# Causal attention with q and k as two float32r parts, two heads side by side in the array, and row maxima running ahead

## The chip, the cores and the metric

One core of a Trainium2 chip runs the whole program. The metric is the device time of one execution in microseconds (us); the kernel before takes 4158.48 us as the median of three runs (4147.53 to 4164.63). PE is TensorE (PEld its weight loads), DVE is VectorE, ACT is ScalarE, POOL is GpSimd, SP the engine whose queue issues nearly all DMAs.

## The reference

Two layers, each `x = x + attention(LN(x)) * silu(ffn(LN(x)))`, on 4 x 2048 tokens of width 256, 16 heads of dimension 16. Layer 0 has dilated, segmented attention and an FFN with fp8 rounding. Layer 1, which the change touches, is:

```python
q, k = _apply_rope(q, k, sin, cos)            # after q = x @ wq.T + bq, and so on
att = jnp.einsum('bhtd,bhsd->bhts', q, k) * (1.0 / np.sqrt(hd))
att = jnp.where(causal[None, None], att, -jnp.inf)
att = jax.nn.softmax(att, axis=-1)
y = jnp.einsum('bhts,bhsd->bhtd', att, v)
return jnp.einsum('btc,dc->btd', y.transpose(0, 2, 1, 3).reshape(B, T, C), wo) + bo
```

Its FFN is a mixture of 8 experts, the top 2 for each token, hidden width 1024. All of it is float32, and the kernel keeps nearly that precision.

## The kernel before

Four phases run one after the other: `layers_phase` (layer 0, and layer 1's norm, q, k, v and router logits, in 16 turns of 512 tokens), `attend_phase` (layer 1's attention), `experts_phase` and a final phase.

**layers_phase.** q and k come out of the rotation in `rot`, and are split into three bf16 pieces whose sum is the float32 value: ACT copies `rot` to piece 0 (`part0`, L565), DVE writes `rot` minus piece 0 back to `qk` (`rest`, L788), ACT copies that to piece 1 (`part1`, L569), POOL subtracts for piece 2 (`last_part`, L345). `store_layer1` writes the pieces to DRAM (L279) in 12 DMAs a turn. Between these, DVE works through the layer 0 part of the next token block: `residual` ends with `x1 = x + ez` (L773), then come norm statistics (L665), quantisation, the block-diagonal keys (L712 to L717, on which PE's `scores` wait).

**attend_phase.** 16 groups (4 batches x 4 quarters of the heads), G = 4 heads each, 2048 tokens. `qs` and `ks` hold, on 96 partitions, six stacked combinations of the pieces (`Q_PIECES`, `K_PIECES`), so that one bf16 matmul over 96 rows gives q times k at float32 precision; three more rows of `qs` hold minus the row maximum, also in three pieces, against ones in `ks`. Each group has two kinds of work:

- *Row scores* (`row_scores`, L1197, causal mask by an identity matmul L1200): queries on partitions, up to 512 keys. Only their maximum is used: DVE reduces each of the 160 chunks of a group (`chunk_max`, L1313) from `p1`, three buffers of one PSUM bank. At the end of the group `negate`, a PE transpose (L1206) and `split` turn the 64 x 128 maxima and split them into three pieces, and three DMAs (`maxima`, L1127) put them under the q rows.
- *Key scores* (`key_scores`, L1217, mask L1220): keys on partitions, queries along the row, in 20 steps of up to two key tiles, a head at a time (80 units) into `st`, two buffers of 1024 columns. ACT takes the exponential of each unit (L1294) into `ex`; the values matmuls (`values`, L1234, float32, the four heads in four column strips of 32) add the sums into `ob`; at each of the four query quarters' ends ACT copies `ob` (L1283), PE turns it (L1244), DVE divides (`normalise`, L1338 and L1341) into one of two `yout` buffers, SP stores it (L1135).

PE's order is written out: while group g does its key scores, the row scores of group g+1 are spread among them by `due_at`, a table from cumulative widths, and values lag one step. The maxima of g+1 are therefore complete only at g's end. The first group's 160 chunks run alone beforehand. SP's queue runs in program order; per group it holds the load of group g+2 (`load`, L1117 and L1120, 24 + 2 DMAs), three stores, the maxima, a fourth store. `normalise` waits until the store of two quarters before has landed.

## Time and profile before

| | us |
|---|---|
| median of three runs | 4158.48 |
| span of the profiled execution | 4106.3 |
| layers_phase | 0 to about 1110 |
| attention's own set-up and first load | about 1110 to 1161 |
| row scores of group 0 alone | 1161 to 1265 |
| 16 groups | 1265 to about 3098 |
| experts and final phase | to the end |

The profile shows one execution. Its span runs from the first to the last instruction; its own total time isn't recorded apart, and the median of the runs lies 52.2 us above the span. Busy times count overlapping instructions of one engine once; a matmul's duration includes the array's latency, so what a matmul costs in a dense stretch is the distance from one start to the next.

### The profile page before, as it was taken

The page shows a single profiled execution, that of the slowest core. Times are in us where ns is not written, and L with a number is a line of the kernel's source. Part 1 is how long each engine was busy: PE and PEld are TensorE (multiplying, and loading weights), DVE is VectorE, ACT ScalarE, POOL GpSimd, SP SyncE. Part 2 cuts the span into 40 slices and gives each one's busy share as a digit, 9 for nine tenths or more (in the row PEclk, how much of TensorE's full clock was granted, in tenths as well). Part 3 has the DMA queues.
Part 4 walks back from the last instruction along what each step waited for, and adds up shares of the span by engine and source line. Part 5 has one row for each costly group of instructions (what it writes and reads, how often), then busy time and mean ns, then how long its engine had stood idle before and what let it go on. Part 6 is the DMA issues. An engine that isn't in the chain of part 4 may idle for free. (4 is left out here: it accounts for less than half of the span.)

```text
span 4106.3 us, 65569 instructions
## 1 busy us (share of the span) xinstructions
PE 3499.3 (85%) x20499; PEld 1877.5 (46%) x20500; DVE 2863.1 (70%) x5100; ACT 1766.9 (43%) x2274; POOL 745.4 (18%) x968
## 2 busy tenths in 40 slices
PE   5777777777359999999999999999997999999954
PEld 2333333343113333333333333333335888888943
DVE  5777776776468777788778778787724665566556
ACT  2333333333103665666566566566673332233211
POOL 0333323233112222100000000000002121111066
PEclk9899888888658999999999999999998999999977
DMA  2121221212232221123333212223002121121077
GB/s 70 45 79 57 67 83 41 82 51 68 78 75 45 48 47 35 25 41 47 48 46 48 48 26 41 39 41 48 7 7 90 58 71 61 66 67 62 32 204 215
DMA packets 261897, 247.41 MB, mean 60 GB/s; under 512 B 92530, under 2 KB 233970, under 8 KB 261306
## 3 DMA queue, kind: packets, MB, share of 16 engines
q1 hardware_dynamic: 245178, 209.58, 21.8%
q0 software_dynamic: 16384, 33.64, 2.8%
q8 instruction: 175, 2.87, 0.3%
q14 instruction: 160, 1.31, 0.1%
HBM read 149.70 MB, written 92.67 MB: 59 GB/s over the span
## 5 line engine op out<-in xcount | busy, mean ns | idle before, releaser
L1313 DVE TENSOR_REDUCE at_part<-at_p 128x1 f32<-128x512 f32 (+3 forms) x2560 | 1402.1, 605 | 310.4 <-PE at_p L1197 192.2
L1294 ACT ACTIVATE at_ex<-at_st 128x1024 f32<-128x1024 f32 (+1 forms) x1280 | 1109.3, 895 | 830.8 <-PE at_st L1220 472.5
L1197 PE MATMUL at_p<-at_ks,at_qs 96*128 96x512 bf16 (+3 forms) x2560 | 838.3, 366 | 89.6 <-DVE at_part L1313 32.8
L1217 PE MATMUL at_st<-at_qs,at_ks 99*128 99x512 bf16 (+3 forms) x2560 | 713.3, 350 | 6.5 <-ACT at_ex L1294 4.9
L1234 PE MATMUL at_ob<-at_ex,at_vs 128*32 128x512 f32 (+3 forms) x5120 | 588.3, 541 | 3.6 <-ACT at_ex L1294 3.5
L1197 PEld LDWEIGHTS at_p<-at_ks,at_qs 96*128 96x128 bf16 x2560 | 248.1, 98 | 688.5 <-DVE at_part L1313 490.4
L1475 POOL DMA_INDIRECT e_xg<-s_xn,e_table x128 | 146.9, 1148 | 1978.2 <-DMA e_table<-s_table 1405.2
L1565 ACT ACTIVATE e_hh<-e_hb,e_b1now 128x512 fp32r<-128x512 f32 x256 | 176.3, 689 | 527.5 <-PE e_hb L1500 498.9
L1217 PEld LDWEIGHTS at_st<-at_qs,at_ks 99*128 99x128 bf16 x2560 | 242.0, 99 | 252.2 <-ACT at_ex L1294 97.8
L1530 PE MATMUL e_ob<-e_w2h,e_hh 128*128 128x256 f32 x1024 | 295.1, 288 | 15.5 <-DVE e_og L1623 15.5
L1532 PE MATMUL e_ob<-e_w2h,e_hl 128*128 128x256 f32 x1024 | 291.7, 285 | 0.0
L1531 PE MATMUL e_ob<-e_w2l,e_hh 128*128 128x256 f32 x1024 | 291.5, 285 | 0.0
L1608 DVE TENSOR_SCALAR e_h<-e_hb,e_b1now 128x512 f32<-128x512 f32 x256 | 191.1, 746 | 57.6 <-ACT e_hh L1565 54.5
L1200 PE MATMUL at_p<-at_mask_q,at_identb 128*128 128x128 bf16 x1024 | 231.1, 228 | 0.0
L598 ACT ACTIVATE a_wexp<-a_shifted 128x512 f32<-128x512 f32 x128 | 80.6, 630 | 329.5 <-DVE a_shifted L726 329.5
L423 PE MATMUL a_sc<-a_qT,a_kbd 128*128 128x512 f32 x256 | 162.9, 736 | 64.3 <-DVE a_vbd L717 63.1
L1623 DVE TENSOR_TENSOR e_og<-e_ob,e_b2now 128x256 f32<-128x256 f32 x128 | 53.7, 424 | 231.7 <-PE e_ob L1532 231.1
L1498 PE MATMUL e_hb<-e_xh,e_w1h 128*128 128x512 f32 x512 | 203.4, 397 | 6.0 <-issue 3.7
L1530 PEld LDWEIGHTS e_ob<-e_w2h,e_hh 128*128 128x128 f32 x1024 | 196.5, 192 | 17.0 <-DVE e_og L1623 17.0
L1500 PE MATMUL e_hb<-e_xh,e_w1l 128*128 128x512 f32 x512 | 203.0, 397 | 0.0
L1499 PE MATMUL e_hb<-e_xl,e_w1h 128*128 128x512 f32 x512 | 202.9, 396 | 0.0
L1220 PE MATMUL at_st<-at_mask_k,at_identb 128*128 128x128 bf16 x1024 | 200.4, 223 | 0.0
(180 smaller groups left out, 4706.9 us busy)
## 6 DMA issues: line engine op xcount, KB each, us to landing
s_qk<-a_piece SPq DMA_DIRECT2D x192, 128.0 KB
at_qs<-s_qk SPq DMA_DIRECT2D x192, 128.0 KB
at_ks<-s_qk SPq DMA_DIRECT2D x192, 128.0 KB
s_v<-a_v SPq DMA_DIRECT2D x64, 256.0 KB, 5.5
at_vs<-s_v SPq DMA_DIRECT2D x32, 512.0 KB
e_w<-w SPq DMA_DIRECT2D x16, 1024.0 KB, 7.5
s_eo<-e_og SPq DMA_DIRECT2D x32, 512.0 KB, 2.6
a_x<-x SPq DMA_DIRECT2D x16, 512.0 KB, 5.2
```

Of the source, the lines that this page charges most:

```text
L1197: last = pe.matmul(out, qs[0:STACK, r, h, qt * P:(qt + 1) * P], ks[0:STACK, r, h, ch * SEG:ch * SEG + w], start=True, stop=not diag)
L1200: last = pe.matmul(out[:, w - P:w], identb[:], mask_q[:], start=False, stop=True)
L1217: last = pe.matmul(out, ks[:, r, h, kt * P:(kt + 1) * P], qs[:, r, h, q0:q0 + w], start=True, stop=not diag)
L1234: last = pe.matmul(ob[h * HW:(h + 1) * HW, SEG - w:SEG], vs[:, r, kt, h * HW:(h + 1) * HW], ex[:, (G * s + h) % NE, at:at + w], start=(kt ...
L1294: ev.done(act.activation(ex[:, u % NE, 0:width], st[:, u % 2, 0:width], ACT.Exp, scale=SCALE), "ex")
L1313: ev.done(dve.tensor_reduce(part[:, at, ch:ch + 1], p1[:, n % NP1, 0:w], AX, ALU.max), "mx")
L1498: pe.matmul(out, ah, bh, start=(j == 0), stop=False)
L1499: pe.matmul(out, ah, bl, start=False, stop=False)
L1500: last = pe.matmul(out, al, bh, start=False, stop=(j == len(pairs) - 1))
L1530: pe.matmul(out, high, w2h[:, u, m, :], start=(m == 0), stop=False)
L1531: pe.matmul(out, high, w2l[:, u, m, :], start=False, stop=False)
L1532: last = pe.matmul(out, low, w2h[:, u, m, :], start=False, stop=(m == HC - 1))
```

## The change

q and k become two float32r parts instead of three bf16 pieces: ACT copies `rot` to part 0, DVE writes `rot` minus part 0 straight to part 1; `part1` and `last_part` are gone. They are stored in 8 DMAs a turn, in a layout with a head's 16 rows together. Loads become 12 + 2 DMAs of 16 rows.

In attention, three stacked combinations (48 rows) plus two rows for the maxima lie at partitions 0 and again at 64, for two heads (a = 0, 1) of a pair; two matmuls, one on rows 0 to 63 and one on rows 64 to 127, follow one another and write different PSUM banks. Masks are matmuls of 64 rows and 64 columns, four for each pair of diagonal tiles instead of two of 128. DVE reduces both heads of a pair with one instruction (up to 128x1024, L1365), from two buffers of two banks; key scores have three buffers of one bank and steps of one key tile (36 steps, 144 exponentials of up to 512 columns instead of 80 of up to 1024), `ex` sixteen buffers. Row maxima are turned a query quarter at a time and run ahead of use: group g's stream holds its own last quarter (0, 3) and the next group's quarters (1, 0), (1, 1), (1, 2), 80 pair chunks and four transposes, and only three quarters of group 0 run alone beforehand. Maxima reach `qs` in eight DMAs a quarter. Values lag one step (two at a quarter's start), and the last values, turn and normalise of group g run in the first two steps of g+1. In SP's queue the last store of group g-1 now stands behind the load of group g+2.

```diff
+        NBUF, NE, NST, NP1 = 3, 4 * G, 3, 2
+        p1 = ps("p1", [P, NP1, PAIRS, SEG])
+        so = ps("so", [P, NST + 1, SEG])
...
+        lead = stream([(0, 0), (0, 1), (0, 2)], [None, (0, 0), (0, 1)])
+        run = stream([(0, 3), (1, 0), (1, 1), (1, 2)], [(0, 2), (0, 3), (1, 0), (1, 1)])
+        tail = stream([(0, 3)], [(0, 2)]) + [("t", 0, 3)]
...
+                def group(g, r, use, first, more):          # SP
+                    items = run if more else tail
+                    maxima(r, 2, g, LEAD + turned_at(items, 0, 2))
+                    if first:
+                        load(slice(2, 3), 2)
+                    else:
+                        if not isinstance(g, int) or g + 2 < NGROUPS:
+                            ev.wait(sp, "pv", g, 0)
+                            sp.sem_inc(passed, 1)
+                            load(bass.ds(g + 2, 1), (r + 2) % NBUF)
+                        output(g - 1, 3)
+                    output(g, 0)
+                    output(g, 1)
+                    maxima(r, 3, g, LEAD + turned_at(items, 0, 3))
...
+                def add_mask(out, mask, a, half, last):
+                    rows = slice(a * HALF, (a + 1) * HALF)
+                    return pe.matmul(out[:, half * HALF:(half + 1) * HALF], mask[rows, half, :], identb[rows, rows],
+                                     start=False, stop=last)
...
+                    for a in range(2):                      # row_scores
+                        rows = slice(a * HALF, a * HALF + STACK)
+                        last = pe.matmul(p1[:, b, a, 0:w], qs[rows, r, p, qt * P:(qt + 1) * P],
+                                         ks[rows, r, p, ch * SEG:ch * SEG + w], start=True, stop=not diag)
...
+                        for a in range(2):                  # key_scores
+                            if i == 0 and (not first or v + a >= NST):
+                                ev.wait(pe, "ex", g, v + a - NST + 1)
+                            rows = slice(a * HALF, a * HALF + ROWS)
+                            last = pe.matmul(so[:, (v + a) % NST, at:at + w], ks[rows, r, p, kt * P:(kt + 1) * P],
+                                             qs[rows, r, p, q0:q0 + w], start=True, stop=not diag)
...
-                def last_part(st, n):
-                    st.mark(pool.tensor_tensor(piece[2][:], qk[:], piece[1][:], ALU.subtract), "p3", n)
-                    st.mark(dve.tensor_tensor(qk[:], rot[:], piece[0][:], ALU.subtract), "rest", n)
+                    st.mark(dve.tensor_tensor(part[1][:], rot[:], part[0][:].bitcast(F32), ALU.subtract), "p2", n)
```

PE in the middle of a group, before: a unit of two key tiles of one head (L1217), single row chunks (L1197), one tile of values (L1234, each row two passes for four heads).

```order
L1217 MATMUL at_st<-at_qs,at_ks 128x512 x2
L85 REGISTER_ALU
L1197 MATMUL at_p<-at_ks,at_qs 128x512
L1200 MATMUL at_p<-at_mask_q,at_identb 128x128
L1234 MATMUL at_ob<-at_ex,at_vs 32x512 x4
L85 REGISTER_ALU
L1197 MATMUL at_p<-at_ks,at_qs 128x512
L85 REGISTER_ALU
L1217 MATMUL at_st<-at_qs,at_ks 128x512
```

PE in the middle of a group, now (L1267 key scores, L1233 row scores, x2 being the two heads of a pair, L1223 masks, L1287 values):

```order
L1267 MATMUL at_so<-at_qs,at_ks 128x512 x2
L1233 MATMUL at_p<-at_ks,at_qs 128x512 x2
L1287 MATMUL at_so<-at_ex,at_vs 32x512 x4
L1267 MATMUL at_so<-at_qs,at_ks 128x512 x2
L1233 MATMUL at_p<-at_ks,at_qs 128x512 x2
L1267 MATMUL at_so<-at_qs,at_ks 128x512 x2
L1233 MATMUL at_p<-at_ks,at_qs 128x512 x2
L1223 MATMUL at_p<-at_identb,at_key_mask 128x64 x4
L1287 MATMUL at_so<-at_ex,at_vs 32x512 x4
```

One tile of values now stands behind two key pairs and two or three row pairs. SP's queue for one group, before (L1135 are the stores, L1127 the maxima):

```order
L1117 DMA at_qs<-s_qk 8x4x2048 x12
L1117 DMA at_ks<-s_qk 8x4x2048 x12
L1120 DMA at_vs<-s_v 128x8x128 x2
L1135 DMA s_y<-at_yout 128x4x64 x3
L1127 DMA at_qs<-at_mT 1x64x128 x3
L1135 DMA s_y<-at_yout 128x4x64
```

SP's queue for one group, now (L1154 maxima, L1141 and L1144 the load, L1160 stores):

```order
L1154 DMA at_qs<-at_mT 1x4x128 x8
L1141 DMA at_qs<-s_qk 16x2x2048 x6
L1141 DMA at_ks<-s_qk 16x2x2048 x6
L1144 DMA at_vs<-s_v 128x8x128 x2
L1160 DMA s_y<-at_yout 128x4x64 x3
L1154 DMA at_qs<-at_mT 1x4x128 x16
L1160 DMA s_y<-at_yout 128x4x64
```

The store that closed a group's rows before is the first of the three behind the load now. DVE in group 0 now, with what it waits for (L1383 begins `normalise`; a group's second one waits for the `yout` buffer that the last store of the group before reads):

```order
L1365 TENSOR_REDUCE at_best<-at_p 128x2 [waits at_s1] x8
L1383 RECIPROCAL at_rden<-at_so 128x16 [waits at_y_out0,at_ot]
L1386 TENSOR_TENSOR at_yout<-at_so,at_rden 128x256 [waits at_rden]
L1365 TENSOR_REDUCE at_best<-at_p 128x2 [waits at_s1] x15
L1383 RECIPROCAL at_rden<-at_so 128x16 [waits at_y_out1,at_ot]
L1386 TENSOR_TENSOR at_yout<-at_so,at_rden 128x256 [waits at_rden]
```

The fifteen reduces between the two are row pairs; the second `normalise` stands in step 11 of 36.

## Rows read from the trace of the kernel before

**Rows 1.** The page: span, and busy time of each engine.

```profile
span 4106.3 us, 65569 instructions
PE 3499.3 (85%) x20499; PEld 1877.5 (46%) x20500; DVE 2863.1 (70%) x5100; ACT 1766.9 (43%) x2274; POOL 745.4 (18%) x968
```

**Rows 2.** Stretches: length, busy us of PE, PEld, DVE, ACT, POOL; clock, DMA share.

```profile
1161.00:1265.00 104.00, 80.82 (x225) 21.24 (x225) 97.80 (x188) 0.00 (x0) 23.85 (x43) 0.50 0.16 38
1500.00:1900.00 400.00, 385.11 (x2711) 153.54 (x2710) 318.45 (x604) 245.57 (x291) 56.43 (x100) 0.99 0.28 47
3010.00:3098.00 88.00, 80.14 (x588) 24.21 (x584) 3.02 (x10) 70.44 (x87) 0.00 (x0) 1.00 0.03 7
```

**Rows 3.** One instruction per group: the maxima's cast, first and last start.

```profile
L1326 DVE CAST at_mT<-at_p x16: 282/283/283, 1260.4 to 3007.1; 64x128 bf16<-64x128 f32 x16
```

**Rows 4.** Timeline of PE in attention and in the experts: start, us, instruction.

```profile
3003.28 0.38 PE L1217 MATMUL at_st<-at_qs,at_ks 99*128 99x512 bf16 x1
3003.50 0.22 PE L1220 MATMUL at_st<-at_mask_k,at_identb 128*128 128x128 bf16 x1
3003.56 0.33 PE L1217 MATMUL at_st<-at_qs,at_ks 99*128 99x384 bf16 x1
...
3004.48 1.07 PE L1234 MATMUL at_ob<-at_ex,at_vs 128*32 128x512 f32 x8
3005.48 0.39 PE L1217 MATMUL at_st<-at_qs,at_ks 99*128 99x512 bf16 x1
...
3300.22 0.39 PE L1498 MATMUL e_hb<-e_xh,e_w1h 128*128 128x512 f32 x1
3300.45 0.40 PE L1499 MATMUL e_hb<-e_xl,e_w1h 128*128 128x512 f32 x1
```

**Rows 5.** DVE's timeline: routing work amid group 0's chunks, one head's 40 chunks.

```profile
1163.56 1.22 DVE L986 COPY r_count<-at_st 128x1024 f32<-128x1024 f32 x1
...
1176.71 19.74 DVE L1313 TENSOR_REDUCE at_part<-at_p 128x1 f32<-128x512 f32 x38
1196.63 20.88 DVE L1313 TENSOR_REDUCE at_part<-at_p 128x1 f32<-128x384 f32 x40 [0.17 <-PE at_p L1200]
```

**Rows 6.** By shape, 1265 to 3007 us: busy, mean ns of one, idle before.

```profile
L1313 DVE TENSOR_REDUCE at_part<-at_p 128x1 f32<-128x512 f32 x1680 | 1096.8, 685 | 226.1 <-PE at_p L1197 191.7 <-PE at_p L1200 25.3
L1294 ACT ACTIVATE at_ex<-at_st 128x1024 f32<-128x1024 f32 x959 | 957.7, 1023 | 677.3 <-PE at_st L1217 343.1 <-PE at_st L1220 325.8
L1283 ACT ACTIVATE at_osb<-at_ob 128x512 f32<-128x512 f32 x59 | 35.0, 593 | 10.6 <-PE at_ob L1234 10.6
```

**Rows 7.** SP's queue in one group, then DMA share and GB/s of its load.

```profile
2541.07 1.77 SPq L1127 DMA_DIRECT2D at_qs<-at_mT  x3
...
2547.70 4.91 SPq L1117 DMA_DIRECT2D at_qs<-s_qk  x12
...
2557.78 27.58 SPq L1120 DMA_DIRECT2D at_vs<-s_v  x2
...
2548.00:2600.00 52.00, 50.43 (x354) 20.22 (x352) 43.83 (x83) 33.19 (x40) 0.00 (x0) 1.00 0.61 89
2568.00:2572.00 4.00, 4.00 (x32) 1.83 (x30) 3.10 (x6) 2.71 (x3) 0.00 (x0) 1.00 0.52 75
```

**Rows 8.** layers_phase: L773's ns min/median/max, and POOL beside the 4.7 us one.

```profile
L773 DVE TENSOR_TENSOR a_x<-a_x,a_ez x16: 1224/4691/4704, 78.8 to 1047.5; 128x1024 f32<-128x1024 f32 x16
725.46 4.70 DVE L773 TENSOR_TENSOR a_x<-a_x,a_ez 128x1024 f32<-128x1024 f32 x1
725.00 4.08 POOL L345 TENSOR_TENSOR a_piece<-a_qk,a_piece 128x2048 bf16<-128x2048 f32 x1 [17.27 <-DMA s_qk<-a_piece]
```

**Rows 9.** First load and first chunk; a stretch behind 12.5 us without matmuls, granted clock.

```profile
1116.60 4.06 SPq L1117 DMA_DIRECT2D at_qs<-s_qk  x12
1161.23 0.29 PE L1197 MATMUL at_p<-at_ks,at_qs 96*128 96x128 bf16 x1 [31.18 <-DMA at_vs<-s_v]
1058.80:1066.90 8.10, 6.83 (x14) 3.75 (x15) 0.00 (x0) 1.77 (x3) 0.00 (x0) 0.50 0.70 218
```

More of the change, by code:

```diff
@@ L1066, in attend_phase, with quarter @@
-        due_at = [min(u for u in range(TURN_AT) if step_work[u + 1] * chunk_work[-1] >= c * step_work[-1])
-                  for c in chunk_work]
-        def due(u):
-            return [n for n in range(NC) if due_at[n] == u]
-        counts = dict(s1=NC, mx=NC, neg=1, negT=1, mT=1, m_in=PIECE, st=NU, ex=NU, pv=NS, oc=SPB, ot=SPB,
+        NV = NS * G
+        ends = [max(s for s in range(NS) if steps[s][0] == qc) for qc in range(SPB)]
+        starts = [0] + [s + 1 for s in ends[:-1]]
+        def quarter(ahead, qc):
+            return [("c", ahead, qc, p, qt, ch) for qt in range(TT * qc, TT * qc + TT)
+                    for ch in range(qc + 1) for p in range(PAIRS)]
@@ new lines, in stream @@
+        def stream(quarters, turned):
+            out = []
+            for (ahead, qc), t in zip(quarters, turned):
+                chunks = quarter(ahead, qc)
+                out += chunks[:2] + ([("t",) + t] if t else []) + chunks[2:]
+            return out
+        lead = stream([(0, 0), (0, 1), (0, 2)], [None, (0, 0), (0, 1)])
+        run = stream([(0, 3), (1, 0), (1, 1), (1, 2)], [(0, 2), (0, 3), (1, 0), (1, 1)])
+        tail = stream([(0, 3)], [(0, 2)]) + [("t", 0, 3)]
+        LEAD, RUN = len(lead), len(run)
@@ new lines, in wide, with due @@
+        def wide(item):
+            return min(SEG, (item[4] + 1) * P - item[5] * SEG) if item[0] == "c" else P // 2
+        FIXED = P // 2
+        step_work = np.cumsum([0] + [steps[u // 2][1][-1][1] + steps[u // 2][1][-1][2] + FIXED for u in range(2 * NS)])
+        item_work = np.cumsum([wide(x) + FIXED for x in run])
+        slot_of = [min(u for u in range(2 * NS) if step_work[u + 1] * item_work[-1] >= w * step_work[-1])
+                   for w in item_work]
+        def due(u, more):
+            return [k for k in range(RUN if more else len(tail)) if slot_of[k] == u]
@@ new lines, in closes, with turned_at, summed_after, sums_after @@
+        def closes(items, k):
+            return items[k][0] == "c" and not any(x[:3] == items[k][:3] for x in items[k + 1:])
+        def turned_at(items, ahead, qc):
+            return items.index(("t", ahead, qc)) + 1
+        def summed_after(s):
+            return s + 2 if s in starts else s + 1
+        def sums_after(s):
+            return [x for x in range(NS) if summed_after(x) == s]
+        counts = dict(s1=RUN, mx=RUN, neg=SPB, mstep=SPB, m_in=G * PART * SPB, st=NV, ex=NV, pv=NS, oc=SPB, ot=SPB,
@@ L1139, in _ @@
                 route.zero_table(sp)
-                maxima(0, 0)
-                def turn(i, loads):
-                    for r in range(NBUF):
-                        g = i * NBUF + r
-                        if r < loads:
-                            ev.wait(sp, "pv", g, 0)
-                            sp.sem_inc(passed, 1)
-                            load(bass.ds(g + 2, 1), (r + 2) % NBUF)
-                        group(g, r, True)
-                NTURN = (NGROUPS - 1) // NBUF
-                with sp.Fori(0, NTURN - 1) as i:
-                    turn(i, NBUF)
-                turn(NTURN - 1, NBUF - 1)
-                group(NGROUPS - 1, 0, False)
+                for qc in range(2):
+                    maxima(0, qc, 0, turned_at(lead, 0, qc))
+                groups(sp, group)
+                output(NGROUPS - 1, 3)
                 for k in range(2):
@@ new lines, in stream_item @@
+                def stream_item(g, r, use, it, n, items, k):
+                    item = items[k]
+                    if n + k >= NP1:
+                        ev.wait(pe, "mx", it, n + k - NP1 + 1)
+                    if item[0] == "c":
+                        if item[1] == 1 and item[1:] == quarter(1, 0)[0][1:]:
+                            ev.wait(pe, f"in{(r + 1) % NBUF}", use, 1)
+                        last = row_scores((r + item[1]) % NBUF, item, (n + k) % NP1)
+                    else:
+                        ev.wait(pe, "neg", g + item[1], item[2] + 1)
+                        last = pe.transpose(p1[:, (n + k) % NP1, 0, 0:P], negmax[:], ident[:])
+                    ev.done(last, "s1")
@@ L1233, in values @@
+                def values(g, r, s):
+                    qc, tiles = steps[s]
+                    ev.wait(pe, "ex", g, G * s + G)
+                    if s in starts:
+                        ev.wait(pe, "norm", g, qc)
+                    for kt, at, w in tiles:
                         for h in range(G):
@@ L1235, in values @@
                                              ex[:, (G * s + h) % NE, at:at + w], start=(kt == 0),
[L1236 to L1239 removed]
+                                             stop=(s in ends and kt == tiles[-1][0]), skip_group_check=True)
+                    ev.done(last, "pv")
                 def turn(g, qc):
@@ L1269, in _ @@
                 route.prefix_sums(pe)
                 ev.wait(pe, "in0", 0, 1)
-                for n in range(NC):
-                    row_scores(0, 0, n)
-                turn_maxima(0)
-                group_loop(pe, group)
+                for k in range(LEAD):
+                    stream_item(0, 0, 0, 0, 0, lead, k)
+                groups(pe, group)
+                values(NGROUPS - 1, (NGROUPS - 1) % NBUF, NS - 1)
+                turn(NGROUPS - 1, SPB - 1)
             @block.scalar
```

377 lines of the change are left out of this document (174 added, 203 removed).

## Prediction

> **What bounds the kernel now.** I read the page first, then a table of stretches, then attention's timeline by engine. The page gives PE 85%, DVE 70%, ACT 43% of 4106.3 us [rows 1], an average over phases with different limits. The stretches tell more: in the group loop PE is busy 385 of 400 us, DVE 318, ACT 246 [rows 2]. The cast that ends each group's maxima starts at 1260.4 us the first time and at 3007.1 the sixteenth [rows 3], so a group takes (3007.1 - 1260.4)/15 = 116.4 us. A busy PE isn't proof, so I price its work by the distance between starts [rows 4]: a 512-column bf16 matmul 0.22 us, a 128-column mask 0.06, one values tile for four heads 1.00 until the next matmul. A group has 224 full score matmuls (48.4 us at 0.216), 96 narrower ones at 0.16, 0.11 and 0.06 (10.6), 128 masks (7.7), 40 values tiles (28 full, 12 narrow, with the gap ahead of each some 38), and four turns at about 0.65 (2.6). That is 107 us of 116.4: PE's own work is the bound, and 9 us go to waits on its neighbours.
>
> **Attention's loop, engine by engine.** All a group's scores are now pairs on two halves of the rows: 112 full pairs and 48 narrow ones. float32r streams 512 columns in 0.23 us [rows 4]; no row of before shows two halves side by side. If they run side by side a full pair costs 0.23, otherwise 0.46. I take side by side, because the values matmuls already do it by columns: eight instructions, two passes each for four heads, end within 1.07 us [rows 4], where one after the other 8 x 0.427 would be 3.4. So 112 x 0.232 = 26.0, and 48 x 0.2 = 9.6 for the narrow ones (between 0.06, a mask's spacing, and 0.23). The 256 quarter masks have no row of their shape: between 0.03 (half of 0.06) and 0.06 each is 7.7 to 15.4; I take 11.5. Values keep 29.0 us of streaming (17,408 columns x 4 passes at 2.4 GHz), with 0.23 around each of 36 calls instead of 40: 37.3. Turns and the four maxima transposes: 3.8. PE's sum is 88 us.
>
> DVE: one head's 40 chunks took 20.88 us back to back [rows 5], so 83.5 a group. A 1024-wide read of PSUM is 1.22 alone, a full chunk 0.685 [rows 5, 6], so 128 columns are 0.134, and from 20.88 a full chunk in a row is (20.88 + 3.2)/40 = 0.60. A full pair in a row is then 1.14. With 56 full pairs (63.6) and 24 narrow ones at 0.87, 0.60 and 0.34 (14.5) the maxima cost 78; normalise, negating and splitting by quarter add 6. DVE's sum is 84. ACT: 128 exponentials of 512 columns, 0.593 as L1283's copy and 0.57 in a row [rows 6], 16 of 256 at 0.35, four copies: 81.
>
> Three engines at 88, 84 and 81 that wait on each other can't reach the largest sum. PE is in order and has to come back to the key pair. A head's second matmul of step s needs the exponential of the first (three buffers), so one step can't be shorter than: key pair to its end 0.40 [rows 4], exponential 0.57, second key pair 0.23, half of the step's row chunks, values 1.08 with the gap. Without the chunks that is 2.28 x 36 = 82; half the row chunks' PE time (13.0 + 4.8 full and narrow, 5.8 masks, 1.2 transposes) adds 12.4, the key masks in twelve steps 3, turns 2.6, less 2 for narrow steps: 98, and since a step has one to five chunks, unevenly, I round up to **100 us a group**, against 116.4.
>
> **A new wait.** `normalise` of quarter 1 stands at the end of step 11 and needs the store of the previous group's quarter 3, which SP now issues behind the load. Step 11 ends after 32.5% of the widths, so at 0.325 x 100 + 1 = 33.5 us. The load: the first transposed maxima are ready at about 4.3 us (step 1), eight DMAs at 0.59 [rows 7] make 8.7. The load now takes 52 us at a DMA share of 0.61, that is 31.7 us of all sixteen engines; while q and k move the share is 0.52 [rows 7], half the engines, with 8 partitions to a DMA. With 16 partitions I take 31.7. The store lands about 3 us behind it, at 43.4. DVE waits 10 us, and behind it in its queue are the row chunks, for which PE waits after two buffers, and ACT after PE. After such a pause PE runs at the lower of its two levels: behind 12.5 us without matmuls it had granted clock 0.50 (1.2 GHz) for 8 us [rows 9]. I add 3 us for that. A group then takes **113 us**, and the loop gains 15 x (116.4 - 113) = 51. The Trainium skill ("DMA: Bandwidth & Descriptors", section on why a DMA increments its semaphore by 16) says that a DMA uses the largest number of engines up to 16 that divides its slowest dimension: 8 before and 16 now. The 0.52 agrees; by the page the load would indeed need half the time for q and k.
>
> **The rest.** *Lead.* From the first chunk to the first key scores it is 1161.2 to 1265.4 = 104 us, DVE-bound (97.8 of 104) [rows 2]. Now 13.1 us of routing work [rows 5], 48 pair items (24 full at 1.14, 24 diagonal in fours of 1.14, 0.87, 0.60, 0.34: 45), 5 for negating, splitting and short bubbles: 63, minus 41. PE is at 0.50 there, where a full pair is 0.43, under DVE's 1.14. *layers_phase.* L773 takes 1.22 us alone and 4.69 in the median, when POOL's L345 runs beside it [rows 8]; L345 is gone. DVE has no idle time from there to the block-diagonal keys, for which PE waits, so 14 turns x 3.4 count: minus 48. ACT's second copy (1.9 us) stood in idle time: nothing. *Its end.* One ACT copy, L345 (4.1) and four DMAs fewer, less what larger DMAs cost: minus 6. *First load.* 1116.6 to 1161.2 = 44.6 [rows 9] becomes 32 + 2, but the three memsets and the ones by DMA start it 3 later: minus 8. *Last group.* 88 us before [rows 2], with PE 80 and ACT 70; the same step chain gives about 88: nothing.
>
> Sum: 51 + 41 + 48 + 6 + 8 = 154; 4106.3 - 154 = 3952. The median of the runs lies 52.2 above the profiled span, so **4004**, say 4000.
>
> **Rivals.**
> *The store's wait doesn't bite* (the load drains faster, or slack in buffers takes it): 100 us a group, 15 x 16.4 = 246 + 103 = 349, giving 3809. For it: a stretch of layers_phase moved 218 GB/s [rows 9], the load 89. Against: the stores stand in order behind 4 MB.
> *The halves don't run side by side.* Pairs cost 33 us more, PE 121, with 7 to 9 of waits 129 a group: +189, the last group +10, -103: 4255, **slower**. It decides from 0.38 us for a full pair on (PE's sum then 105 to 110 and a group above 123). For it: no row shows row halves. The Trainium skill ("TensorE: Matmul & The Clock Gate", "Measured speedup vs the span model") gives 3.07 times for four row tiles, so it speaks against this rival; by it a pair would be close to 0.23.
> *The load keeps its 52 us pace.* The store lands at 8.7 + 52 + 3 = 64, DVE waits 30 us, a group takes up to 133 with the clock's 3: 4300 at most, **slower**; it decides from about 40 us of load on, where a group takes 121 to 124. For it: 512-byte rows of v hold the queue 27.6 us even now [rows 7].
> *Tighter coupling*: bursts of three narrow chunks with masks in one step and two values tiles in another; 106 instead of 100: 4060.
> *The change doesn't do what it says* would show as pairs in sequence, the second rival. That PE falls to 1.2 GHz for the whole loop, as in the lead at 0.50 with PE waiting for each chunk [rows 2], would cost hundreds; I give it 3%.
>
> **How the numbers follow.** 4000 has 0.42, the first rival 0.24, tighter coupling 0.08, faster than all 0.04; halves in sequence 0.11, the slow load 0.08, the clock 0.03. The forecast's own range is 3930 to 4060. 3770 to 4180 leaves out the worst of the slow cases and the fastest. Faster by more than 0.5% (what a measurement can tell here) 0.79, same 0.05, slower 0.16.
>
> **What would show it.** Pairs of L1267 and L1233 starting within hundredths of each other, pairs 0.23 apart; L1365 at 1.14 us; the spacing of the maxima casts about 113; once a group, near a third of it, an idle stretch of 8 to 12 us on DVE ahead of L1383 that a store ends, and the clock low behind it; L773 at 1.2 in every turn; a lead of 63. Wrong would be: pairs 0.46 apart, no such idle stretch, or a DMA share that stays at 0.5.

## The result, and the profile after

The changed kernel takes 4312.5 us (median of 4 runs, 4277.1 to 4321.2) against 4161.6 us for the kernel before in the same set: ratio 1.035, 95% interval 1.030 to 1.040. It is **slower by 3.5%**; 4000 us had been forecast, with 3770 to 4180 as the range. In a later set, on another chip, the ratio was 1.026 (1.023 to 1.029).

The page of the changed kernel: span, busy time, then PE's busy share and the granted clock in 40 slices [beside rows 1]. The profiled execution's own time is 4277.1 us.

```profile
span 4275.2 us, 67161 instructions
PE 3545.4 (83%) x22596; PEld 2019.3 (47%) x22596; DVE 2761.8 (65%) x3918; ACT 1788.8 (42%) x3282; POOL 678.5 (16%) x952
...
PE   5777777875498998999998898889987999999745
...
PEclk9899998997579998778779999996987999999867
```

No engine has a higher busy share than before, and in the loop the clock goes down to 7 tenths where it was 0.99 [rows 2]. Next, one source line each (ns min/median/max, first and last start): DVE's addition in layers_phase, row pairs, key pairs.

```profile
L761 DVE TENSOR_TENSOR a_x<-a_x,a_ez x16: 1224/1224/1226, 79.0 to 1010.2; 128x1024 f32<-128x1024 f32 x16
L1233 PE MATMUL at_p<-at_ks,at_qs x2560: 215/436/793, 1107.0 to 3145.2; 48*128 48x512 f32 x137, 48*128 48x128 f32 x20, 48*128 48x384 f32 x20, 48*128 48x256 f32 x20
L1267 PE MATMUL at_so<-at_qs,at_ks x2560: 275/494/793, 1169.6 to 3217.9; 50*128 50x512 f32 x139, 50*128 50x384 f32 x20, 50*128 50x256 f32 x19, 50*128 50x128 f32 x19
```

These date every part. The first row chunk starts at 1107.0 instead of 1161.2 [rows 9], the first key pair at 1169.6 instead of 1265.4: **95.8 us gained** before the loop. From the first key scores to the last the kernel before needs 1265.4 to 3094.7, 1829.3 us; now it is 2048.3: **219 us lost** in the loop, 187 of them in the fifteen stretches of the next section, 17 ahead of these and 15 behind. What follows attention is the same code in both and took 46 us longer here, nearly all in the last phase. As far as the sets tell, that goes by the chip: they fall into chips with the kernel before at 4162 to 4178 us and the time behind the last `normalise` at 1046 to 1064, and chips with 4109 to 4120 and 1005 to 1019. The profile of before, with 1009, fits the latter. -96 + 219 + 46 = 169, the difference of the two spans.

### The profile page after: what moved, and what is told of

The parts are those of the page before. It is cut to its first block and busy times, and to the rows that moved or that the text cites. A ratio compares the mean times of both kernels' runs of the same rounds, so it can differ in the third digit from the quotient of the medians.

```text
span 4275.2 us, 67161 instructions
## 1 busy us (share of the span) xinstructions
PE 3545.4 (83%) x22596; PEld 2019.3 (47%) x22596; DVE 2761.8 (65%) x3918; ACT 1788.8 (42%) x3282; POOL 678.5 (16%) x952
## 5 line engine op out<-in xcount | busy, mean ns | idle before, releaser
L1365 DVE TENSOR_REDUCE at_best<-at_p 128x2 f32<-128x1024 f32 (+3 forms) x1280 | 1336.8, 1064 | 557.7 <-PE at_p L1233 372.5
L1341 ACT ACTIVATE at_ex<-at_so 128x512 f32<-128x512 f32 (+1 forms) x2304 | 1164.1, 576 | 962.5 <-PE at_so L1267 560.6
L1267 PE MATMUL at_so<-at_qs,at_ks 50*128 50x512 f32 (+3 forms) x2560 | 854.1, 492 | 95.5 <-ACT at_ex L1341 68.8
L1233 PE MATMUL at_p<-at_ks,at_qs 48*128 48x512 f32 (+3 forms) x2560 | 709.6, 460 | 106.6 <-DVE at_best L1365 62.4
L1267 PEld LDWEIGHTS at_so<-at_qs,at_ks 50*128 50x128 f32 x2560 | 382.1, 205 | 738.3 <-ACT at_ex L1341 546.0
L1287 PE MATMUL at_so<-at_ex,at_vs 128*32 128x512 f32 (+3 forms) x5120 | 671.7, 621 | 36.7 <-DVE at_yout L1386 36.4
L1233 PEld LDWEIGHTS at_p<-at_ks,at_qs 48*128 48x128 f32 x2560 | 325.4, 210 | 152.7 <-DVE at_best L1365 108.0
L1569 PE MATMUL e_ob<-e_w2h,e_hh 128*128 128x256 f32 x1024 | 293.6, 287 | 15.6 <-DVE e_og L1662 15.6
L1287 PEld LDWEIGHTS at_so<-at_ex,at_vs 128*32 128x32 f32 x5120 | 124.7, 117 | 251.0 <-issue 154.9
L712 DVE TENSOR_REDUCE a_keymax<-a_sc 128x8 f32<-128x512 f32 x128 | 88.2, 689 | 167.5 <-PE a_sc L417 166.0
L1570 PEld LDWEIGHTS e_ob<-e_w2l,e_hh 128*128 128x128 f32 x1024 | 195.1, 191 | 0.0
```

The costliest lines, as they stand in the source:

```text
L1233: last = pe.matmul(p1[:, b, a, 0:w], qs[rows, r, p, qt * P:(qt + 1) * P], ks[rows, r, p, ch * SEG:ch * SEG + w], start=True, stop=not diag)
L1267: last = pe.matmul(so[:, (v + a) % NST, at:at + w], ks[rows, r, p, kt * P:(kt + 1) * P], qs[rows, r, p, q0:q0 + w], start=True, stop=not diag)
L1287: last = pe.matmul(ob[h * HW:(h + 1) * HW, SEG - w:SEG], vs[:, r, kt, h * HW:(h + 1) * HW], ex[:, (G * s + h) % NE, at:at + w], start=(kt ...
L1341: ev.done(act.activation(ex[:, v % NE, 0:width], so[:, v % NST, 0:width], ACT.Exp, scale=SCALE), "ex")
L1365: ev.done(dve.tensor_reduce(best[:, at:at + TT * PAIRS + 1:TT * PAIRS, ch], p1[:, (n + k) % NP1, :, 0:wide(item)], AX, ALU.max), "mx")
L1569: pe.matmul(out, high, w2h[:, u, m, :], start=(m == 0), stop=False)
```

## Where the loop's time goes

**Groups at different clocks.** A table of stretches, each from one group's third reciprocal (L1383, the start of a `normalise`) to the next one's, five of fifteen: length, busy us of PE, PEld, DVE, ACT, POOL, clock, DMA share, GB/s.

```profile
1643.10:1785.80 142.70, 132.05 (x919) 60.88 (x920) 89.09 (x101) 74.34 (x148) 12.05 (x21) 0.74 0.25 35
...
1917.10:2056.30 139.20, 129.32 (x918) 58.84 (x920) 88.69 (x100) 74.55 (x148) 0.00 (x0) 0.76 0.25 35
...
2319.50:2439.70 120.20, 107.68 (x919) 49.98 (x918) 88.13 (x101) 74.05 (x149) 0.00 (x0) 0.94 0.29 41
...
2562.80:2681.40 118.60, 105.62 (x919) 48.62 (x919) 88.09 (x102) 74.01 (x149) 0.00 (x0) 0.97 0.28 42
...
2801.10:2936.90 135.80, 124.11 (x918) 56.09 (x917) 88.84 (x101) 74.55 (x149) 0.00 (x0) 0.80 0.26 37
```

The same program takes 118.6 to 142.7 us, longer the lower the clock. The granted clock is 1.0 (2.4 GHz) or 0.5 (1.2 GHz), so a mean of 0.74 over 142.7 us is about 73 us at 1.2 GHz. Over all fifteen the mean is 127.5 us with 32.4 at 1.2 GHz; a straight line through the fifteen gives 115.6 + 0.37 for each low microsecond. I call 115.6 the full-clock group. Before, the fifteen average 115.1, the last, without row scores for a next group, included. So there are two losses to explain: full-clock groups that are no shorter than before, and 12 us a group for the clock.

**A step at the full clock.** PE, ACT and DVE in one step with two row chunks, one behind each key pair.

```profile
2585.61 0.50 PE L1267 MATMUL at_so<-at_qs,at_ks 50*128 50x512 f32 x2
...
2585.94 0.40 PE L1233 MATMUL at_p<-at_ks,at_qs 48*128 48x512 f32 x2
...
2586.14 2.07 ACT L1341 ACTIVATE at_ex<-at_so 128x512 f32<-128x512 f32 x4 [1.38 <-PE at_so L1267]
2586.18 0.40 PE L1267 MATMUL at_so<-at_qs,at_ks 50*128 50x512 f32 x1
2586.39 2.39 DVE L1365 TENSOR_REDUCE at_best<-at_p 128x2 f32<-128x1024 f32 x2 [0.97 <-PE at_p L1233]
2586.79 0.18 PEld L1267 LDWEIGHTS at_so<-at_qs,at_ks 50*128 50x128 f32 x1 [0.65 <-ACT at_ex L1341]
2586.79 0.50 PE L1267 MATMUL at_so<-at_qs,at_ks 50*128 50x512 f32 x1 [0.21 <-ACT at_ex L1341]
...
2586.88 0.64 PE L1233 MATMUL at_p<-at_ks,at_qs 48*128 48x512 f32 x2
...
2587.44 1.06 PE L1287 MATMUL at_so<-at_ex,at_vs 128*32 128x512 f32 x8
2588.44 0.19 PEld L1267 LDWEIGHTS at_so<-at_qs,at_ks 50*128 50x128 f32 x2 [0.84 <-ACT at_ex L1341]
```

The first pair is side by side (x2, ended within 0.50 us). The second is not: its first half starts at 2586.18, its second at 2586.79, when the exponential of the step's first head frees the third buffer, and the row chunk behind it is pulled apart with it. Round the step: key pair to exponential 0.53, exponential and hand-over 0.65, second half of the key pair and of the chunk 0.65, values 1.00: **2.83 us**. DVE and ACT both idle in it.

**The load.** The load of one group in the table of stretches (columns as above), then PE's timeline in it.

```profile
1968.00:1976.00 8.00, 7.32 (x67) 3.78 (x59) 6.35 (x9) 5.14 (x11) 0.00 (x0) 1.00 0.64 91
1976.00:1994.00 18.00, 17.05 (x155) 7.40 (x155) 13.50 (x13) 11.51 (x25) 0.00 (x0) 1.00 1.04 121
1994.00:1998.20 4.20, 0.11 (x3) 0.03 (x2) 0.17 (x1) 1.51 (x3) 0.00 (x0) 0.72 0.96 103
1998.20:2010.00 11.80, 11.80 (x51) 5.52 (x50) 6.94 (x8) 4.54 (x9) 0.00 (x0) 0.50 0.48 111
2010.00:2040.00 30.00, 29.61 (x165) 12.84 (x162) 15.22 (x20) 12.05 (x24) 0.00 (x0) 0.50 0.00 1
...
2067.00:2090.00 23.00, 20.32 (x148) 8.19 (x148) 18.33 (x20) 14.61 (x29) 0.00 (x0) 0.99 0.01 2
...
1998.17 0.48 PE L1233 MATMUL at_p<-at_ks,at_qs 48*128 48x384 f32 x1 [4.09 <-issue]
```

PE stands 4.09 us between the two matmuls of one pair, where nothing in the program makes it wait ("issue"), and the clock is 0.50 from there to 2067, 72 us in all. What it waited for shows by DMA queue: the 25 us before the pause, and the 28 before those.

```profile
q1 hardware_dynamic: 536, 2.89, 95.0%
```

```profile
q8 instruction: 3, 0.05, 0.9%
q14 instruction: 2, 0.02, 0.2%
q1 hardware_dynamic: 40, 0.01, 0.2%
```

I read queue 8 as the one that brings PE's code: it moves blocks of 16 KB, mostly every 10 to 20 us. While q and k of the load take 95% of the sixteen engines none comes, for 26 us (1968.5 to 1994.8), and PE runs dry; the block of 1994.8 lands at 1996.6, and PE goes on at 1998.17. In the kernel before the load had 57% of the engines, and code blocks came. The Trainium skill ("DMA: Bandwidth & Descriptors", section "Queues, rings and completion order") has each engine take turns between the queues that have work for it; by that alone a block would not be held up for so long. The times here show that it is held up, though not to the load's end: v's 1 MB moved until 2006, with another block, at 2002.3, amid it. That the missing block is what PE waited for is inferred from these times; e16 below tests it. Two other things mark a group: the wait of normalise for the store, and PE's pause of 1.2 us in step 27 of all fifteen groups, where two 128-column chunks stand behind a full one and PE waits for DVE. And the pauses are not all of the clock's story: of the 486 us at 1.2 GHz in the fifteen stretches some 200 begin where PE has not stood for over 1 us, most of them in steps 4 and 15, three times for 41 us on end. For the wait of normalise, what ended the idle time before L1383 (us, times):

```profile
  DMA s_y<-at_yout: 44.0, 11
```

## The experiments

"Group" is the mean of the fifteen distances as above, "low" the part of it at 1.2 GHz, "full" the straight line's value at no low clock (left out where nearly every microsecond was low). Ratios are to the kernel before, measured in the same set; the sets ran on different chips, so ratios are compared, not times.

| kernel | ratio (95%) | group | low | full |
|---|---|---|---|---|
| changed | 1.035 (1.030 to 1.040) | 127.5 | 32.4 | 115.6 |
| e14_again, the same | 1.026 (1.023 to 1.029) | 129.9 | 41.0 | 115.1 |
| e1_store_first | 1.029, medians alone | 129.5 | 43.1 | 116.2 |
| e2_cols | 1.017 (1.010 to 1.023) | 126.9 | 45.7 | 106.4 |
| e4_double_first | 1.016 (1.012 to 1.020) | 122.9 | 13.2 | 114.7 |
| e6_same_half | 1.313 (1.305 to 1.321) | 206.2 | 179.3 | |
| e7_cols_store | 0.998 (0.993 to 1.002) | 122.7 | 37.7 | 106.8 |
| e8_cols_one | 1.040 (1.035 to 1.045) | 133.1 | 45.1 | 113.4 |
| e9_cols_both | 1.053 (1.049 to 1.057) | 136.5 | 36.0 | 120.0 |
| e11_spread | 1.017 (1.012 to 1.021) | 125.7 | 31.9 | 114.8 |
| e12_cols_spread | 1.013 (1.009 to 1.017) | 124.5 | 41.2 | 105.5 |
| e13_cols_early | 0.983 (0.979 to 0.986) | 117.8 | 27.6 | 102.5 |
| e16_after_six | 1.026 (1.022 to 1.029) | 128.4 | 44.0 | 112.8 |
| e18_place | 0.979 (0.973 to 0.985) | 113.1 | 9.6 | 109.0 |
| **e15_six** | **0.942 (0.940 to 0.943)** | 107.1 | 10.6 | 101.2 |
| e17_unroll | 0.942 (0.939 to 0.944) | 106.1 | 9.2 | 101.5 |

### Are the halves side by side? e6_same_half

```diff
-    rows = slice(a * HALF, a * HALF + STACK)     # row pairs; key pairs and masks alike
+    rows = slice(0, STACK)
```

> The changed kernel with both heads of every pair, and both mask halves, on the first 64 rows of the array, so that they run one after the other (this leaves out the second head's scores: its columns are computed from the first head's rows). If the halves run side by side in the changed kernel, each full pair now costs 0.43 to 0.46 instead of 0.23 to 0.33 where it doesn't wait: 10 to 25 us a group more, 4470 to 4700. Rival, they never overlapped in time although they start together: no difference, 4280 to 4340.

Ratio 1.313: the halves do run side by side in the changed kernel, and this rival of the prediction is dead. The loss, 79 us a group, is far above the 10 to 25 expected, since the clock was low nearly throughout. The stretch 1400 to 2600 of this kernel:

```profile
1400.00:2600.00 1200.00, 1187.32 (x5190) 633.22 (x5183) 510.39 (x569) 433.15 (x839) 67.73 (x120) 0.55 0.17 25
```

PE is busy 1187 of 1200 us, and the clock is 0.55. A PE that never stands can still be at 1.2 GHz.

### The step: e2_cols, and doubled work: e4_double_first, e8_cols_one, e9_cols_both

e2 cuts the 512-column values tile into two times 256 columns and puts one part between the step's key pairs. (It cuts a quarter's first tile too, and so leaves part of that tile's sums out; from e7 on that tile is whole.)

```diff
 for p in range(PAIRS):
     key_scores(g, r, s, p, first)
     for k in due(2 * s + p, more):
         stream_item(g, r, use, g, LEAD, items, k)
...
-for x in sums_after(s):
-    values(g, r, x)
+    for x, part in (halves[:cut], halves[cut:])[p]:
+        values(*x, part)
```

> The changed kernel with the values tile of a 512-column step cut into two times 256 columns, one between the step's two key pairs and one behind the second (in the five steps that hold a quarter's first tile everything stays behind). Return-path theory: the exponential of the first head is done by the time PE comes to the second key pair, both its halves start together, and a two-chunk step falls from 2.85 us to 2.2 to 2.4 at the full clock; a group from 116 to 98 to 104, and the whole to 3980 to 4130, with a clock above 0.87 since PE waits less. Rival, PE's own work is the bound of the step (PE is busy 90% of the stretch 2500 to 2700): 28 more matmul groups with a start of their own each make a group 0 to 5 us longer, 4310 to 4390.

The full-clock group fell from 115.6 to 106.4, so the wait for the exponential was the bound of a step, though the 98 to 104 expected weren't reached. And the low clock rose to 45.7 us and ate most of the gain: a group took 126.9 us, the whole 4236, above the expected range.

e4 computes a row pair twice where PE was thought to wait.

```diff
-    last = row_scores((r + item[1]) % NBUF, item, (n + k) % NP1)
+    for _ in range(times):      # 2 for the first chunk behind the first key pair
+        last = row_scores((r + item[1]) % NBUF, item, (n + k) % NP1)
```

> The changed kernel with the first row-score chunk behind the first key pair of each step computed twice (same output, 0.25 us of PE work more in nearly every one of 36 steps, 8 to 9 us a group). Return-path theory: it lies in the 0.61 us between the two halves of the second key pair, during which PE waits for the exponential, so the group stays within 3 us: 4290 to 4360. Rival, PE's sum is the bound: +8 to 9 us a group, 4440 to 4460. If it is too little PE activity that lets the clock fall, the clock rises above 0.87 here.

More work made it **faster** than the changed kernel, by 1 to 2% (1.016 against 1.026 and 1.035 in two sets), outside the range expected: free at the full clock (114.7 for 115.6), and the low clock down to 13.2 us. From this I took a simple theory, that the clock follows the amount of work, and tried it on the cut version.

> The same with the first row-score chunk behind the first key pair of each step computed twice, as extra work for PE (0.25 us, about 30 times a group; same output). Clock theory: the low clock falls from 40 to 55 us a group to 5 to 20, which gives back 10 to 18 us, against 4 to 7 us of added PE time in steps that DVE bounds: a group 111 to 118, the whole 4060 to 4140. Rival, work and clock are not tied (the doubled chunk helped the changed kernel in another way): the added work costs 30 x 0.25 = 7 us a group and the time rises by 100 over the run without it.

> The same with the first chunk behind each of the two key pairs of a step computed twice (about 65 of a group's 80 chunks). Clock theory: the clock is low for under 5 us a group, but now 14 to 16 us of PE time are added, and a half step becomes 0.5 + 0.34 + 0.33 + 0.25 = 1.4 us instead of 1.24: a group 117 to 122, the whole 4130 to 4200, slower than with one chunk doubled. Rival as above: 4330 or more.

It fell: one doubled chunk adds 7 us to the full-clock group, as priced, and the low clock goes up, not down (45.1 for 37.7 us; with two chunks doubled it is 36.0). The place of the falls says more than the sum of work. In e8 and e9 the clock falls behind pauses of PE in steps 7 to 10 (1.8 to 6.6 us, waiting for code), in step 27 (1.1 us) and at the loop's turn, and behind step 27 it stays low up to 61 us. Why doubling shortened these stretches in e4 and not here stays open.

### The store and the load: e1_store_first, e7_cols_store, e11_spread, e12_cols_spread, e16_after_six

```diff
-load(bass.ds(g + 2, 1), (r + 2) % NBUF)
 output(g - 1, 3)
+load(bass.ds(g + 2, 1), (r + 2) % NBUF)
```

> The changed kernel with one edit: in each group SP issues the store of the previous group's quarter 3 ahead of the load of the group after next. The wait of normalise (L1383) for that store, 44.0 us in 11 groups of the changed kernel's trace, should vanish, and with it PE's 36.4 us at the values matmuls. Return-path theory (the loop is slower because a step's second key pair waits for the exponential of its first, and because the granted clock falls): only these 36 to 44 us go, the clock stays near 0.86, 4312 becomes 4260 to 4280. Rival, the store wait as the root, whose pauses let the clock fall for the rest of the group: the low clock goes too (about 500 us of the loop at 1.2 GHz, which cost some 12 us a group), and the time comes to 4080 to 4130.

The wait for the store went wholly, the time hardly: median 4287.2 (4218 to 4321, too wide for an interval), 1.029 of the kernel before in its set, between the 1.026 and 1.035 of the changed kernel. The low clock stayed (43.1 us; its profile is of the run with 4321). With the cut values on top:

> The changed kernel with both edits so far: values of 512 columns cut in two, one part between the step's key pairs (a quarter's first tile stays whole and behind), and the store of quarter 3 ahead of the load. Clock theory (PE's granted clock falls the more, the less matmul work the array does per time): at the full clock a group takes 103 to 107 us as in the run with the cut values (106.4 extrapolated to no low clock), but 40 to 55 us of each group are at 1.2 GHz, so a group comes out at 122 to 127 and the whole at 4190 to 4240. Rival, the clock fell there because of the pauses at the store's wait: with these gone a group takes 105 to 112 and the whole 3980 to 4060.

0.998, 37.7 us of low clock: the store's pauses were not the root. Against e2 (1.017, 45.7) something was gained; how much of it comes from the store and how much from the whole first tile isn't separated. Next, v's halves apart from q and k, behind the stores of quarters 0 and 1, in the changed kernel and in the cut version.

> The changed kernel with one edit: the load of the group after next is no longer issued in one piece. q and k stay where they are, the first half of v goes behind the store of quarter 0, the second behind that of quarter 1, so the store of quarter 3 follows q and k at once. Theory (the load at a DMA share of 1.0 holds back PE's code and the store; PE stands 1.4 to 9.2 us in steps 11 and 12 of 13 groups, and each pause is followed by a stretch at the low clock): these pauses go, the low clock falls from 32 us a group to 12 to 20, a group from 127.5 to 118 to 122, and the ratio to before from 1.035 to 0.995 to 1.015. Rival, the clock falls from too little work in the array and the pauses only mark the place: the low clock stays at 28 to 40 us a group and only the pauses' 3 us go, ratio 1.02 to 1.03.

> The kernel with the cut values and the early store (122.7 us a group with 37.7 at the low clock, 106.8 extrapolated to none), with v loaded as two pieces in the same way. By the theory the pauses of 3.4 to 6.4 us in steps 7 to 10 go with the 20 us of low clock behind each; those of step 27 (0.8 us) and of the loop's turn stay: low clock 15 to 25 us, a group 112 to 117, ratio 0.955 to 0.975 instead of 0.998. Rival: unchanged clock, ratio 0.985 to 1.00.

Both missed; e12 is even above e7 (1.013 for 0.998). PE's pauses stayed (1.4 to 4.4 us in step 11; 2.8 to 6.8 in steps 7 to 10), since q and k alone still come in one burst: the code blocks are mostly 23 to 29 us apart there, and mostly 10 to 19 elsewhere. So the load in six pieces in the changed kernel, with the store of quarter 3 ahead of them (condensed):

```diff
+def piece(k):
+    load(bass.ds(g + 2, 1), (r + 2) % NBUF, [k])   # q, k of half 0, 1; v's halves
 maxima(r, 2, g, ...)
+output(g - 1, 3); piece(0)
-load(bass.ds(g + 2, 1), (r + 2) % NBUF)
-output(g - 1, 3)
-output(g, 0); output(g, 1)
+output(g, 0); piece(1); output(g, 1); piece(2)     # 3 to 5 behind the next three
```

> The changed kernel with one edit: the load is issued as six pieces of 0.5 or 0.75 MB (q of each half, k of each half, v's two halves) at six places of the group instead of at one, behind steps 2, 5, 12, 16, 20 and 23; the store of quarter 3 stands ahead of them. Theory (the load in one burst holds back PE's code and the store): no gap of over 20 us between two code blocks, no pause of PE over 1.4 us except at the loop's turn, step 27's 1.2 us stays; low clock 32 to 41 us a group becomes 12 to 22, a group 118 to 122, ratio to before 0.985 to 1.005 instead of 1.026 to 1.035. Rival (the clock falls for lack of work, wherever): pauses go but the low clock stays above 28 us, ratio 1.01 to 1.025.

Half right. The pauses of over 1 us in steps 3 to 26 of the fifteen groups are gone, so the load in one burst was their cause. Moving the store alone, as e1 and e7 do, had ended only those that wait for it. But the time is no better (1.026), and 44.0 us of a group are at the low clock: it falls in step 15 (12 times in 15 groups, against 4 in the changed kernel), 4 and 27, and stays down 3 to 55 us, most often 41. The stretches around one such step, and DVE in it:

```profile
1858.00:1866.00 8.00, 7.56 (x57) 2.80 (x56) 6.80 (x6) 4.87 (x10) 0.00 (x0) 1.00 0.84 116
1866.00:1869.00 3.00, 2.27 (x25) 1.35 (x21) 2.27 (x5) 2.07 (x4) 0.00 (x0) 0.94 0.00 0
1869.00:1895.00 26.00, 25.62 (x157) 11.94 (x159) 11.31 (x17) 9.86 (x20) 0.00 (x0) 0.50 0.24 36
...
1866.45 1.23 DVE L1374 TENSOR_REDUCE at_best<-at_p 128x2 f32<-128x1024 f32 x1 [0.52 <-PE at_p L1232]
1867.71 0.22 DVE L1379 TENSOR_REDUCE at_negmax<-at_best 128x16 f32<-128x64 f32 x1
1867.85 0.75 DVE L1374 TENSOR_REDUCE at_best<-at_p 128x2 f32<-128x256 f32 x2
1868.85 0.28 DVE L1384 CAST at_mT<-at_p 64x128 fp32r<-64x128 f32 x1 [0.25 <-PE at_p L1261]
...
1869.41 0.69 DVE L1374 TENSOR_REDUCE at_best<-at_p 128x2 f32<-128x512 f32 x1
```

Step 15 has a full chunk, two of 128 columns, a transpose and one of 256 in a row. Two buffers tie PE to DVE's pace there, so PE has a few narrow matmuls in 3 us, and the clock falls at the end.

### Work beside the narrow chunks: e13_cols_early, e18_place

```diff
-    for k in due(2 * s + p, more):
+    mine = due(2 * s + p, more)
+    for k in mine[:1]:
         stream_item(g, r, use, g, LEAD, items, k)
...
+    for k in mine[1:]:
+        stream_item(g, r, use, g, LEAD, items, k)
```

> As the one before, and in each half step the values part stands behind the first row chunk instead of behind all of them, so that PE has work while DVE reads a wide chunk ahead of narrow ones (step 27: PE waited 0.8 us there in each group of the loop, and the low clock began behind it in 8 of 15 groups and lasted up to 51 us). By the theory the falls at step 27 go: low clock under 15 us, a group 108 to 113, ratio 0.94 to 0.96. Rival, a pause of 0.8 us is not what lets the clock fall: low clock as in the one before, difference under 0.5%.

No clock falls at step 27 are left but one at 28 in group 0, and the ratio goes from 1.013 to 0.983 (low 41.2 to 27.6 us, less than hoped: the load's pauses were still there). e18 does the same to e16, with the values whole:

> The changed kernel with the load in six pieces (ratio 1.0255, 128.4 us a group, 44.0 of them at the low clock, 112.8 extrapolated to none) and one more edit: a step's values stand whole behind the first row chunk of its second key pair instead of behind all chunks (in steps 27 and the like, with three chunks behind the first key pair, behind the first of these). Theory (the clock falls where the narrow chunks come one behind the other with PE waiting for DVE between them): the falls in steps 15 and 27 go, the low clock comes to 5 to 18 us a group, a group to 113 to 119, ratio 0.97 to 0.995. Rival, only the cut values (fewer waits of the key pair for the exponential) keep the clock: low clock above 30 us, ratio 1.01 to 1.03.

Low clock 44.0 to 9.6 us, ratio 1.026 to 0.979, within the range expected; no fall in step 15, two left from step 28, and short ones (3 to 17 us) in step 20. **It was the place of the values**, behind the first chunk, where they give PE work while DVE reads. (The full-clock group fell too, from 112.8 to 109.0.)

### Both together: e15_six and e17_unroll

> The version with cut values behind the first row chunk (117.8 us a group, 27.6 of them at the low clock, ratio 0.983, 102.5 extrapolated to none), with the load in six pieces. Theory: the pauses of 3 to 6 us in steps 7 to 10 of 11 groups go and with them 14 to 24 us of low clock each: low clock 5 to 12 us a group, a group 105 to 110, ratio 0.935 to 0.96. Rival: low clock stays above 22 us, ratio 0.97 to 0.985.

> As e15_six, with PE's 16 groups written out instead of a loop over three groups at a time, so that PE's program has no jump. Theory: PE's pauses of 2.7 to 3.3 us at the loop's turn (groups 3, 6, 9) and the 14 us of low clock behind each are gone: 4 x (3 + 5) = 20 to 30 us less than e15_six. Rival: without the loop the code comes no sooner, difference within 10 us.

3881.8 us against 4120.4: **5.8% faster than the kernel before**, some 8 to 9% faster than the changed one. Its page and a two-chunk step:

```profile
span 3885.2 us, 73305 instructions
PE 3342.3 (86%) x25668; PEld 1952.1 (50%) x25668; DVE 2751.8 (71%) x3918; ACT 1809.1 (47%) x3282; POOL 680.5 (18%) x952
...
PEclk9898999989759999989999999999979999999977
```

```profile
1973.86 0.50 PE L1276 MATMUL at_so<-at_qs,at_ks 50*128 50x512 f32 x2
...
1974.20 0.40 PE L1242 MATMUL at_p<-at_ks,at_qs 48*128 48x512 f32 x2
...
1974.53 0.64 PE L1301 MATMUL at_so<-at_ex,at_vs 128*32 128x256 f32 x8
1974.64 2.46 DVE L1386 TENSOR_REDUCE at_best<-at_p 128x2 f32<-128x1024 f32 x2 [0.68 <-PE at_p L1242]
...
1975.10 0.50 PE L1276 MATMUL at_so<-at_qs,at_ks 50*128 50x512 f32 x2
...
1975.44 0.40 PE L1242 MATMUL at_p<-at_ks,at_qs 48*128 48x512 f32 x2
...
1976.34 0.50 PE L1276 MATMUL at_so<-at_qs,at_ks 50*128 50x512 f32 x2
```

This step is 2.48 us, and both key pairs are whole (x2 in 0.50). PE goes from start to start in 0.34 + 0.33 + 0.57 = 1.24 us for half a step, without a pause, and DVE takes 1.23 for a chunk. Over the loop PE is the nearer to its bound: from 1400 to 2600 us it is busy for 1166, DVE for 978. Writing PE's groups out (e17) brought nothing that shows: the pauses at the turn mostly went, but with them only 1.4 us of low clock a group.

### The layers phase: e10_before_short

```diff
-st.mark(pool.tensor_tensor(piece[2][:], qk[:], piece[1][:], ALU.subtract), "p3", n)
+st.mark(pool.tensor_tensor(piece[2][:, :, :, 0:8], qk[:, :, :, 0:8], piece[1][:, :, :, 0:8],
+                           ALU.subtract), "p3", n)
```

> The kernel before with one edit: POOL's subtraction that makes the third part (L345, 4.1 us) works on 8 of 512 columns only, the other columns of that part stay zero (so the third part is left out nearly whole). My reading of the layers phase: L773 on DVE takes 4.69 us because that operation runs beside it; it falls to 1.2 to 1.5 us in every turn, and 14 turns x 3.4 = 48 us of the phase go: 4165 becomes 4110 to 4125. Rival, another operation of POOL takes its place beside L773, or DVE was not on the path there: L773 stays above 3 us or the time stays within 10 us of 4165.

```profile
L775 DVE TENSOR_TENSOR a_x<-a_x,a_ez x16: 1224/1224/1226, 78.6 to 1006.6; 128x1024 f32<-128x1024 f32 x16
```

In this run POOL's operation works on 8 of 512 columns, and DVE's took 1.22 us in every turn: POOL's was what stretched it to 4.69 us [rows 8]. The time went from 4117.8 to 4080.1 (ratio 0.992, 0.989 to 0.994): 38 us instead of 48, and the last start moved by 41.

## Why the prediction was wrong, by its steps

- **Layers phase, its end, first load** (-48, -6, -8): the first chunk starts 54 us earlier, for 62. Right mechanism, a little oversized; L773's 3.4 us in 14 turns gave 38 to 41.
- **Lead** (63 us): 1107.0 to 1169.6 is 62.6. Right.
- **Halves side by side**: right, by e6. But "a full pair costs 0.23" holds only in part: behind the values, where a pair's weight load starts together with it (PEld at 2585.60, matmul at 2585.61), the next pair follows after 0.33, where it follows after 0.24 in mid-row (2585.94 to 2586.18), and the second key pair of each step doesn't start as a pair at all.
- **The step chain** is the term that failed in the full-clock group. It had the right shape, and the three buffers in it, but summed to 2.51 with one chunk (0.40 + 0.57 + 0.23 + 0.23 + 1.08), where 2.83 is measured: 0.53 from the pair to the exponential, not 0.40; 0.65 with the hand-over, not 0.57; 0.65 for the halves behind it, not 0.46; 1.00 for the values. An estimate from this one step, 0.32 x 36 = 11.5, covers most of the 15.6 us between the 100 forecast and the 115.6 found. The rest may be with the bursts of narrow chunks, for which the prediction had rounded up by 2; that wasn't measured apart.
- **The new store wait** exists, but is 44.0 us in 11 groups instead of 10 in each; e1 shows that its removal alone changes little.
- **The load** got faster as forecast: a share of 1.0 and 121 GB/s for 0.61 and 89 [rows 7], and that of the group above over in 35 us (1971 to 2006) for 52. What was not asked is what else uses those engines. With the sixteen full, PE's code came late.
- **Last group** was put at nothing: behind the last third reciprocal the loop takes 15 us more than before, and ahead of the first one 17 more.
- **The clock** had 3 us a group and a 3% rival "for the whole loop". It cost 12 a group, 0.37 x 32.4; without these the kernel would have come to some 4130 us (an estimate, 4312 - 15 x 12), about the time of the kernel before. The step that failed here is the reading of [rows 9], that low clock comes once a group, behind the store's pause, and costs 3 us. The kernel before showed 7 us of low clock behind the 3.5 us at its loop's turn; in the changed kernel a fall behind 1 to 5 us lasts up to 75, and others come with no such pause.

So two terms failed, the step chain and the clock. In all 113 was forecast for a group and 127.5 came: +15.6 for the step, +12 for the clock, -13 for the stall and its clock that had been allowed for. Of the rivals the slow load (4300 at most) and the halves in sequence (4255) came nearest in time, each for a reason that didn't hold. Tighter coupling (106 for 100) named the right place and too small a size, and PE at 1.2 GHz "for the whole loop" held for a quarter of it. A gain of the size forecast was there to be had, but only with further changes: e15 is at 0.942, the forecast was 4000/4158 = 0.962.

Not settled: why the low clock lasts 7 us in one group and 40 to 75 in another with the same program, and what the doubled chunk does in e4 that it doesn't in e8. The falls are tied to pauses and narrow stretches by e16, e13 and e18; how long they last was only watched.

## What to carry to other kernels

Sum a chain of waits from rows in which the waits occur (start of one to start of the next, hand-over included), not from durations of undisturbed instructions: 0.3 us in a step was, by the estimate above, 10% of this loop. When work in the array gets shorter, look at what the clock will do where PE runs thin, and put dense work (here the value sums) behind the first of several narrow, reader-bound chunks. And spread a bulk load over the loop: here, filling all sixteen DMA engines in one burst kept PE's own code away. Spreading it paid only once the clock no longer fell for other reasons (nothing in e16, 4% from e13 to e15).

## What the runs showed of the hardware

- Across a burst of loads (95 to 104% of sixteen engines) the 16 KB blocks read as PE's code came 22 to 31 us apart in the changed kernel, and PE, waiting for nothing in the program, stood up to 4.1 us there and 6.8 us in e12; with the load in six pieces no such pause was left but at the loop's turn (2.9 to 4.1 us).
- The clock fell to 1.2 GHz and stayed there 41 us, four times in the changed kernel, where PE had not stood for over 1 us; PE was busy 29.6 of 30 us (2010 to 2040) and the clock still 0.50.
- PE busy 99% of the time, its score matmuls on 48 to 50 of 128 rows, ran at a mean clock of 0.55 (e6).
- Doubling some matmuls made a kernel 1 to 2% faster, with less low clock (13.2 for 32.4 and 41.0 us a group) and the full-clock group unchanged (114.7 for 115.6 and 115.1); in e8 the same doubling did not.
- Two matmuls on the two row halves, where neither has to wait for a buffer, start within hundredths of a microsecond and end together: x2 in 0.50 us.
